# Rounding on ScalarE instead of VectorE, and three numbers of the slot plan, in a fused cross-attention and expert kernel

## The reference

```python
def _qdq(x):                       # int8 fake-quantisation of each row
    s = jnp.maximum(jnp.max(jnp.abs(x), axis=-1, keepdims=True) / 127.0, 1e-08)
    return jnp.clip(jnp.round(x / s), -127.0, 127.0) * s
...
q = _qdq(x) @ _qdq(wq).T + bq                     # x is the layer-normed input
kv = cond @ wkv.T + bkv                           # cond: the context, 1601 rows
attn = softmax(einsum('bnhd,bmhd->bhnm', q, k) * scale)
o = einsum('bhnm,bmhd->bnhd', attn, v)
out = _qdq(o) @ _qdq(wp).T + bp
...
x = x + attention(layernorm(x), ctx, ...)
x = x + experts(layernorm(x), ...)
```

## Time and profile before

| | |
|---|---|
| time, median of three runs | 2124.7 us (2123.26 to 2127.67) |
| the profiled execution's own time | 2119.61 us |
| its span | 2117.9 us |
| PE busy over the span | 1814.9 us (86%) |
| DVE busy | 1780.5 us (84%) |
| ACT busy | 1355.6 us (64%) |
| POOL busy | 896.5 us (42%) |
| mean granted clock | 0.949 of full speed |

### The profile page before, as it was taken

The page is one execution under the profiler, slowest core; times in us unless marked ns, Lnnn a source line. Parts: engine busy times, 40 slices in busy tenths (PEclk is TensorE's granted clock), DMA queues, the critical chain, the costliest instruction groups (busy, mean ns, idle before and its releaser), DMA issues. The chain is left out here.

```text
span 2117.9 us, 60219 instructions
## 1 busy us (share of the span) xinstructions
PE 1814.9 (86%) x24715; PEld 1256.0 (59%) x24774; DVE 1780.5 (84%) x2382; ACT 1355.6 (64%) x1953; POOL 896.5 (42%) x727
## 2 busy tenths in 40 slices
PE   2699999989989998999899989989995216999996
PEld 1577766666757666766666666767773103555553
DVE  4699999979989998999899989979996495666665
ACT  3478776867768777877787777868776342323322
POOL 2123632643363347225532642363334201676776
PEclk9899999999999999999999999999997557999998
DMA  5313323232333233323323231332220254566785
GB/s 159 111 28 85 112 66 77 82 105 53 82 99 95 54 99 98 96 56 100 91 78 78 82 117 41 82 102 76 74 57 26 86 159 144 179 197 225 239 263 184
DMA packets 151922, 224.31 MB, mean 106 GB/s; under 512 B 33188, under 2 KB 86436, under 8 KB 151648
## 3 DMA queue, kind: packets, MB, share of 16 engines
q1 hardware_dynamic: 127760, 164.27, 26.8%
q0 software_dynamic: 22016, 55.60, 8.4%
q10 hardware_dynamic: 1872, 0.55, 0.1%
HBM read 130.32 MB, written 70.79 MB: 95 GB/s over the span
## 5 line engine op out<-in xcount | busy, mean ns | idle before, releaser
L814 DVE TENSOR_TENSOR a_p_low<-a_p 128x1024 f16<-128x1024 f32 (+1 forms) x896 | 1094.2, 1250 | 112.8 <-ACT a_p L661 106.5
L661 ACT ACTIVATE a_p<-ps_s 128x1024 f32<-128x1024 f32 (+1 forms) x896 | 860.1, 966 | 299.2 <-PE ps_s L467 282.3
L467 PE MATMUL ps_s<-a_q_stack,a_k_stack 96*128 96x512 f16 (+1 forms) x1664 | 515.7, 385 | 16.2 <-ACT a_p L661 16.2
L584 PE MATMUL ps_o<-a_v,a_p 128*128 128x65 f16 (+1 forms) x6656 | 449.4, 195 | 35.1 <-DVE a_p_low L814 14.1
L584 PE MATMUL ps_o<-a_v,a_p_low 128*128 128x65 f16 (+1 forms) x6656 | 449.0, 195 | 0.4 <-issue 0.4
L584 PEld LDWEIGHTS ps_o<-a_v,a_p 128*128 128x128 bf16 (+1 forms) x6656 | 354.7, 99 | 125.7 <-DVE a_p_low L814 34.3
L504 PEld LDWEIGHTS ps_p<-wkv,a_ctx 128*128 128x128 f16 x4992 | 318.5, 98 | 145.2 <-DVE a_v L829 21.8
L504 PE MATMUL ps_p<-wkv,a_ctx 128*128 128x128 f16 x4992 | 364.2, 220 | 29.5 <-DVE a_k_parts L820 14.9
L486 PE MATMUL ps_p<-a_ctx,wkv 128*128 128x384 f16 (+2 forms) x1536 | 357.2, 340 | 35.0 <-POOL a_ctx L383 21.7
L584 PEld LDWEIGHTS ps_o<-a_v,a_p_low 128*128 128x128 f16 (+1 forms) x6656 | 318.8, 98 | 0.5 <-issue 0.5
L486 PEld LDWEIGHTS ps_p<-a_ctx,wkv 128*128 128x128 f16 x1536 | 150.0, 99 | 185.4 <-issue 34.6
(11 more groups left out here) (229 smaller groups left out, 2108.1 us busy)
## 6 DMA issues: line engine op xcount, KB each, us to landing
a_k_stack<-a_k_parts SPq DMA_DIRECT2D x378, 80.0 KB, 2.1
d_ys<-f_y SPq DMA_DIRECT2D x71, 256.0 KB
a_ctx_raw<-in_ctx_dram SPq DMA_DIRECT2D x64, 192.0 KB, 2.8
a_q_stack<-d_q_t SPq DMA_DIRECT2D x96, 128.0 KB, 3.6
a_xm<-in_x_dram SPq DMA_DIRECT2D x8, 1024.0 KB, 6.1
d_q_t<-a_q_parts SPq DMA_DIRECT2D x32, 256.0 KB, 3.0
d_q_full<-a_xm SPq DMA_DIRECT2D x32, 256.0 KB, 3.2
a_x_in<-in_x_dram SPq DMA_DIRECT2D x32, 256.0 KB, 3.1
```

The source lines that it names most:

```text
L467: mm = pe.matmul(t["ps_s"][s % 2][0:r, n * N:(n + 1) * N], t["k_stack"][v % 2][0:TERMS * DH, j, kt * P:kt * P + r], t["q_stack"][v % 2][0: ...
L584: mm = pe.matmul(t["ps_o"][:, q * VC:(q + 1) * VC], part[0:r, n * N + q * P:n * N + (q + 1) * P], val, start=(g == 0 and n == 0 and low == ...
L661: act.activation(t["p"][s % NP][0:r, 0:len(tiles) * N], t["ps_s"][s % 2][0:r, 0:len(tiles) * N], ACT.Exp, scale=float(DH) ** -0.5 / WSCALE ...
L814: dve.tensor_tensor(t["p_low"][s % NP][0:r, 0:n], full, high, ALU.subtract).then_inc(lows, 1)
```

## The change

Both multiply-and-round operations leave VectorE and become a ScalarE activation: scale is the row's multiplier, bias a new constant column `toround`. New waits go with them: ScalarE waits for the multipliers (`q_scaled`, `scaled`), and VectorE, before it overwrites a multiplier, for the last batch's rounds. In the plan, the four query projections stand 6 slots apart instead of 4 (and all that follows each of them moves along), the scales' row is loaded at slot 58 instead of 43, and the context blocks of batches 1 to 7 stand 2, 2, 3 and 4 slots sooner (their loads too).

```diff
             if main:
                 self.put("sx_store", b, 0, at + 36)
-                self.put("sx_load", b, 0, at + 43)
+                self.put("sx_load", b, 0, at + 58)
...
-                self.put("q_project", b, kb, at + (82 + 4 * kb if main else FIRST_QUERIES[kb]))
+                self.put("q_project", b, kb, at + (82 + 6 * kb if main else FIRST_QUERIES[kb]))
...
-                    at = (NBLK * b - 2) * SLOTS + 14 + 7 * r + (0, 2, 3, 5)[c] if b else FIRST + FIRST_CONTEXT[r]
+                    at = (NBLK * b - 2) * SLOTS + (12, 19, 25, 31)[r] + (0, 2, 3, 5)[c] if b else FIRST + FIRST_CONTEXT[r]
...
+                for b, m in plan.at("q_round", s):
+                    act.wait_ge(q_scaled, 2 * b + 2)
+                    act.activation(t["xm"][:, m, :], t["xm"][:, m, :], ACT.Identity, bias=t["toround"][:, 0:1],
+                                   scale=t["q_mul"][:, m:m + 1]).then_inc(q_rounded, 1)
...
+                for b, m in plan.at("round", s):
+                    act.wait_ge(scaled, b + 1)
+                    act.activation(t["o_full"][b % 2][:, m, :], t["o_full"][b % 2][:, m, :], ACT.Identity,
+                                   bias=t["toround"][:, 0:1], scale=t["o_mul"][:, m:m + 1]).then_inc(rounded, 1)
...
+            dve.memset(t["toround"][:, :], ROUND)
...
+                    if b >= 1:
+                        dve.wait_ge(q_rounded, b * QT)
                     dve.tensor_tensor(t["q_mul"][:, :], t["tmp"][:, :], t["q_rstd"][:, :], ALU.mult).then_inc(q_scaled, 1)
...
-                for b, m in plan.at("q_round", s):
-                    dve.tensor_scalar(t["xm"][:, m, :], t["xm"][:, m, :], t["q_mul"][:, m:m + 1], ROUND, ALU.mult,
-                                      ALU.add).then_inc(q_rounded, 1)
...
-                    done(dve.reciprocal(t["o_mul"][:, :], t["so"][:, :]))
-                for b, m in plan.at("round", s):
-                    o = t["o_full"][b % 2][:, m, :]
-                    dve.tensor_scalar(o, o, t["o_mul"][:, m:m + 1], ROUND, ALU.mult, ALU.add).then_inc(rounded, 1)
+                    if b >= 1:
+                        dve.wait_ge(rounded, b * QT)
+                    dve.reciprocal(t["o_mul"][:, :], t["so"][:, :]).then_inc(scaled, 1)
+                    dve.wait_ge(scaled, b + 1)
```

More of the change, by code:

```diff
@@ L312, in attention_pass @@
         q_out = [sem(f"a_q_out{n}") for n in range(2)]
+        scaled = sem("a_scaled")
         first_split = sem("a_first_split")
@@ L1103, in attention @@
         t["sx_row"], t["unround"] = sb("sx_row", [P, N]), sb("unround", [P, 1])
+        t["toround"] = sb("toround", [P, 1])
         t["gate_raw"] = sb("gate_raw", [P, CC, E])
```

## The result

The changed kernel takes 2109.9 us (median of 4 runs, 2109.21 to 2110.97) against 2125.74 us (4 runs beside it): a ratio of 0.9928, 95% interval 0.9912 to 0.9944. It is faster by 15.8 us, about a third of the 50 us forecast, and the time lies above the range of 2045 to 2105 us. The profiled execution took 2110.97 us, its span is 2109.3 us.

What follows compares the result with a forecast made beforehand. VectorE was taken as the bound in most slots, TensorE close behind. Terms -38 - 24 + 8 + 4 = -50 us took the profiled 2119.6 to 2069.6; with the median 5.1 us higher, forecast 2075 us, 8-in-10 range 2045 to 2105.

Steps and rivals of the forecast that it cites:

- the context blocks moved sooner: Slots before `q_high`: block 11 moves ahead of POOL's `norm` chain, so SP is no longer held; no term of its own.
- the stop: ScalarE idle before `q_high` in batches 2 to 7, waiting for a held store, 44.1 us; removing it gives -38 us.
- D: Rival: the stop before `q_high` stays, the store being held by something else on SP; 2113 us, chance 0.05.
- B: Rival: TensorE sets the pace once the stops are gone, rounds leaving VectorE worth nothing; 2099 us, chance 0.16.
- The rounds, -24: `o_full` and `xm` rounds in attention slots: 31.7 us counted off VectorE, 0.75 passed through, -24 us.
- my third: Rounds on VectorE: of the 15.6 us between mean and minimum times, a third was counted as leaving.
- The rounds on ScalarE, 0: Rounds of 734 ns, 5.9 us a batch, on a ScalarE with room; cost taken as nothing.
- a case without cover: `q_round` in slot 36: ScalarE's multiplier wait, 1.8 us in 7 batches, not hidden by VectorE's work; 13 us.
- The query load, +8: Next batch's `xm` load on SP comes later, VectorE waits 1.3 us in each of 6 batches; +8 us.
- The `norm` chain, +4: POOL's chain, slowed once VectorE runs on without the stop, makes ScalarE wait in some batches; +4 us.

Runs made afterwards that it cites:

- e11: Changed kernel with a fifth raw buffer and the last two groups' context loads one slot earlier: 2077.96 us, ratio 0.9779 to the kernel before.
- e2: Kernel before with the three plan numbers of the changed kernel, rounds left on VectorE: 2172.56 us, ratio 0.9995 to the kernel before.
- e3: Changed kernel with the context blocks back in their old slots: ratio 0.987 to the kernel before.
- e4: Changed kernel with the query projections 4 slots apart again: ratio 0.9837 to the kernel before.
- e14: Changed kernel with a fifth raw buffer alone, every load at its old slot: 2120.4 us, ratio 0.9812 to the kernel before.
- e12: e11 with the query projections 4 slots apart again: 2110.3 us, ratio 0.9777 to the kernel before.
- c0: The changed kernel run and profiled once more, nothing altered, as control: ratio 0.9941 to the kernel before.
- e1: Kernel before with only the rounds moved to ScalarE, plan as before: 2160.35 us, ratio 0.9943 to the kernel before.
- e13: e11's plan, buffer and loads with the rounds on VectorE: 2127.29 us, ratio 0.9852 to the kernel before.
- e9: e8's plan with the rounds on VectorE: ratio 0.9966 to the kernel before.
- e8: Changed kernel with projections 4 slots apart and the third and fourth context groups 2 slots later: ratio 0.9889 to the kernel before.
- e7: Changed kernel with both rounds on 8 of 512 columns and no rounding constant, values not quantised: ratio 0.9931 to the kernel before.
- e6: Changed kernel with the queries' rounding (`q_round`) two slots later: ratio 0.9942 to the kernel before.

## Why the prediction was wrong, point by point

- *The failed step: the context blocks moved sooner.* I used them once, as help against the stop, and gave them no term. Their loads moved with them, and costing each moved transfer against what stands ahead of it on its queue would have found it: block 11's load is now the first behind the twelve stack transfers, with 6 slots to go, about 12 us, of which held buffers and the stack's issue take 11.7. The measured cost is 30 us in slots 80 to 93 (table above), most of the 35 us between 2075 and 2109.9, and e11 takes 35 us of slots 80 to 107 away again. In e2, with the rounds on VectorE, it is 17 us: in three of the seven batches the load leaves SP 8.2 to 9.0 us into slot 80, and slots 80 to 107 take only 46.3 to 47.0 us. That e2 came out level is due as much to slots 31 to 44, 14 us longer than before; the granted clock is 0.88 or 0.89 in slots 31 to 37 of four of its batches and of one before. Why, no run shows. None of my rivals had it: D's and B's times (2113 and 2099 us) lie about the result, but the stop is gone and TensorE did not set the pace where the gain was lost.
- *The stop, -38:* right in mechanism and size. The wait's row is gone, and slots 94 to 100 gave 37 us. One of the two moves would have been enough: e3 and e4 each lack one and have no stop.
- *The clock:* no word of it stands in the prediction. The longest pause of TensorE in slots 80 to 93 and the granted clock in slots 87 to 93, by batch, read from the timelines and windows: changed kernel, pauses of 3.1 to 4.9 us, clock below 1 in six of seven batches (0.78 to 0.87); e4, 1.8 to 3.7 us, five of seven, but 0.86 throughout; e14, 1.3 to 2.8 us, only one of seven (the longest pause, 0.78); e11 and e12, at most 1.7 us, none. A pause of 3.65 us was followed by no fall (c0, batch 3) and one of 1.87 us by a fall to 0.86 (e4, batch 4), so the length alone doesn't decide it. The trace of before had the same thing in the stop's own slots, a mean clock of 0.83 or 0.84 in slots 94 to 100 of five batches, which I left unread.
- *The rounds, -24:* right in kind, mis-sized. Four pairs of kernels measure it: e1 against before 12 us, the changed kernel against e2 14 us by their ratios, e13 against e11 15.5 us, e9 against e8 17 us. My sum took 31.7 us off VectorE and let 0.75 of it through. Over the attention, from the first head copied out to the last, VectorE's busy time fell by 27.8, 14.5, 20.4 and 18.9 us in these pairs. So I took too much off in all four, and of what did leave VectorE, between 0.4 (e1 against before) and nearly all (the changed kernel against e2) reached the time. In slots 59 to 65 of batch 5 TensorE is busy for 11.70 of 11.70 us after the change, so there rival B's mechanism holds, in part of the slots. In all pairs part of the rounds' time stayed as longer `a_p_low`, which grew from 1100.9 to 1120.5 us over the change. By the port rule of the Trainium skill (SBUF: State Buffer, the section on the two separate sides) only the undisturbed 26.5 us would leave, and the term would be -20; all four pairs agree with this better than with my third, but none isolates the port, and in three even less left.
- *The rounds on ScalarE, 0:* right as far as e7 tests it. They take 813 ns, not 734. ScalarE's wait for the multipliers is 13.1 us in 7 pieces, as large as I had said of a case without cover; e6 moves it away and nothing changes.
- *The query load, +8:* the wait is right, `a_st` waits 7.2 us in 5 pieces for `a_xm`. Less of it reaches the end: slots 10 to 16, behind it, are 0.42 us longer (11.72 to 12.14 us), 3 us in seven batches, and 11.72 again in e4.
- *The `norm` chain, +4:* did not come. Its wait is 14.1 us in 2 pieces, and in the kernel before it was 14.5 us in 2. But e8 shows what the chain can do from POOL's queue to the blocks behind it.
- *Open:* slots 38 to 44 are about 1 us longer with six slots between projections than with four in some batches (11.86 against 10.85 us in batch 5 of the changed kernel and of e4). I did not find why; e11 against e12 says that it is lost in the scatter. The third number of the plan, the scales' row loaded at slot 58, was put back only together with the others (e1), so its own part is not known.

## What to carry to other kernels

When an edit moves work in a plan, write down each transfer that moves with it, and for each the queue it is issued on, what is issued ahead of it, and the buffer it waits for; a slot that is free on the engines can be the worst one on a queue. Cost a stall of some microseconds at more than its length, since TensorE's clock can fall behind it (here 3.6 us for a fall); and read the clock of the kernel before in the same slots. When an operation that was stretched leaves an engine, count its undisturbed time, not its mean: of 47 to 48 us of rounds, 30 undisturbed, 18 to 32 us left VectorE over the whole run, and part of the rest went to its neighbours.

## What the runs showed of the hardware that I had not expected

- The granted clock fell behind pauses of TensorE as short as 1.87 to 2.24 us (e4), and in other batches not behind one of 3.65 us (c0). A fall cost 3.6 us over slots 80 to 107: 53.0 us in the mean of 15 batches with it, 49.4 us in 3 without.
- A full-row activation with scale and bias from f32 to f32 took 813 ns (797 to 831) on ScalarE, against 473 ns for the same work undisturbed on VectorE; on 8 columns it still took 393 ns.
- Twelve small transfers took SP 6.6 to 9.7 us to issue in the changed kernel (64 groups, median 8.5 us, their own waits included), and the load behind them leaves only then.
- The same kernel took 2126.04 to 2172.65 us on different chips, 2.2%, the difference being in the experts' part (345 us on one, 382 to 384 us on two others); ratios to it agreed within 0.0013 (0.9928, 0.9941, 0.994).
